# Reordering the linear attention of two images in the tail of a vision tower kernel

## The chip, the cores and the metric

The kernel runs on one core of one Trainium2 chip. The metric is the device time of one execution in microseconds, the median over runs. Engines are named PE (TensorE), DVE (VectorE), ACT (ScalarE), POOL (GpSimd) and SP (SyncE, which only issues transfers here).

## The reference

Two images of 32 channels, 128 by 128, go through a patch embedding (256 tokens of width 128), two transformer layers with linear attention, a last norm and a head of width 192. After that come one more linear attention with 12 heads of width 16, and one feed-forward block, both with residual sums. The change touches the last attention and what stands just ahead of it:

```python
h = _ln(x, lnf_g, lnf_b) @ head_w + head_b          # the head, 192 wide
# then, on the layer norm of h:
qkv = x_ @ W_qkv                                    # 192 -> 3 * 192
q, k, v = jnp.split(qkv, 3, axis=-1)
q = elu(q) + 1 ; k = elu(k) + 1                     # the features
kv = jnp.einsum('bshd,bshm->bhdm', k, v)
z = 1.0 / (jnp.einsum('blhd,bhd->blh', q, k.sum(axis=1)) + EPS)
out = jnp.einsum('blhd,bhdm,blh->blhm', q, kv, z)
h = h + (out @ W_out + b_out)
```

## The kernel before, in words

Every matmul is laid out for 128 partitions; an image is two tiles of 128 tokens. The program is written out by hand, one list of instructions per engine, with semaphores between them; no scheduler changes the order. An engine takes its list in the order written, and a wait in front of an instruction holds everything behind it on that engine.

The two images are interleaved. In the tail, image 0 is some steps ahead of image 1. For each image `i` the steps are:

- last norm: DVE adds the feed-forward result (`add_ff`), takes moments (`moments`, `mean_and_variance`), and centres (`centre`); PE transposes (`turn`, L327), a gain is multiplied on (`gain`, L1519, on ACT before), PE multiplies by the head (`head`, L440); POOL computes the inverse deviation (L1782), and DVE scales and adds the head's offset (`head_rows`, L1023), which gives `h`.
- norm of `h`: `moments3`, `mean_and_variance`, `centre` on DVE; `turn3` (L332) on PE. The transposed rows are split in a rounded high part and a low part (`high_part3`, `rest_low_part3`, `low_part3` on DVE, one copy of a rest on ACT), so that fast matmuls give full precision.
- projection: `qk3_high` and `qk3_low` give queries and keys of a tile in one bank, `v3_rows` the values.
- features: elu + 1 is computed as max(min(exp, 1), x + 1): `phi3_exp` (L1551) and `phi3_plus_one` (L1555) on ACT read the bank, `phi3_max` (L1037) on DVE joins them. The inverse deviation is applied as their scale.
- attention: `turn_heads` transposes queries, `context3` is keys times values, `context3_masked` and `context3_sums` (DVE) keep the blocks of each head, `numerators3` multiplies by the queries; `denominator3`, `inverse3`, `attention3` (DVE) divide; `turn_heads` again, a copy on ACT, and `attend3` (L489) is the output projection.

Then follow the residual sum, another norm and the feed-forward block (`fc3`, `proj3`), image 0 first.

Semaphores that matter below: `centred3`, `high3`, `low3` (norm and parts of an image are ready), `qk3_done`, `phi3_exp_ready`, `phi3_plus_one_ready`, `phi3_ready`, `context3_ready`, `attention3_ready`, `attention3_columns` (the copy in front of `attend3`).

Of the kernel before, what the change touches and what calls it, by code (L numbers as in the profile page):

```python
# [8 lines left out]
ALU = mybir.AluOpType  # L9
# [6 lines left out]
TOKENS = (SIDE // PATCH) ** 2  # L16
# [8 lines left out]
E = 192  # L25
# [32 lines left out]
def build(nc, small, convb, norm_rows0, norm_rows1, embed0, patches1, qkv_w, rest_w, rows, mix, fc_w, proj_w,  # L58
          head_w, aqkv_w, aout_w, out):
    with ExitStack() as ctx:  # L60
# [3 lines left out]
        def sem(name):  # L64
            return ctx.enter_context(nc.semaphore(name))
# [58 lines left out]
        def bias_row(name, n=0, width=D):  # L124
# [128 lines left out]
            sem(n) for n in ("y_ready", "y_turned",))  # L253
        consts_set = sem("consts_set")
# [52 lines left out]
        def _(pe):  # L307
# [518 lines left out]
            qk3_low(0, 0).then_inc(qk3_done, 1)  # L826
            pe.wait_ge(centred_last, 4)
            turn(TURNF_BANK[1], xn[1]).then_inc(last_turned, 1)
            qk3_low(0, 1).then_inc(qk3_done, 1)
            pe.wait_ge(head_in_ready, 2)  # L830
            head(1, 0).then_inc(head_done, 1)
            head(1, 1).then_inc(head_done, 1)
            v3_rows(0, 0).then_inc(v3_done, 1)
            v3_rows(0, 1).then_inc(v3_done, 1)
# [4 lines left out]
            pe.wait_ge(centred3, 4)  # L839
            pe.wait_ge(q3_columns, 1)  # L840
            turn3(TURN3_BANK[1], TURN3_REST_BANK[1], xn[1]).then_inc(turned3, 1)
            pe.wait_ge(context3_ready, 2)
            numerators3(0).then_inc(numerators3_done, 1)
            pe.wait_ge(high3, 2)
            qk3_high(1, 0)
            pe.wait_ge(low3, 2)
            qk3_low(1, 0).then_inc(qk3_done, 1)
            qk3_high(1, 1)
            pe.wait_ge(attention3_ready, 2)
            turn_heads(AT3_BANK[0], att3[0]).then_inc(attention3_turned, 1)  # L850
            qk3_low(1, 1).then_inc(qk3_done, 1)
# [75 lines left out]
        def _(dve):  # L927
# [106 lines left out]
            def rest_low_part3(i, bankof):  # L1034
                return low_part(yT3_rest[i][EB:P, :], bankof[0:EB, 0:TOKENS], yT3_rest[i][0:EB, :])

# [373 lines left out]
            centre(1, 1, x, D).then_inc(centred_last, 1)  # L1410
            dve.wait_ge(phi3_plus_one_ready, 1)
            phi3_max(0, 0).then_inc(phi3_ready, 1)
# [5 lines left out]
            dve.wait_ge(phi3_exp_ready, 2)  # L1418
            phi3_max(0, 1).then_inc(phi3_ready, 1)
            head_rows(1, 1).then_inc(h_ready, 1)  # L1420
            dve.wait_ge(moments3_done, 3)
# [8 lines left out]
            dve.wait_ge(context3_done, 1)  # L1430
            context3_masked(0).then_inc(context3_ready, 1)
            context3_sums(0).then_inc(context3_ready, 1)
            dve.wait_ge(turned3, 2)
            high_part3(1, TURN3_BANK[1]).then_inc(high3, 1)
            dve.wait_ge(rest_high3, 2)
            rest_low_part3(1, TURN3_REST_BANK[1])
            dve.wait_ge(high3, 2)
            low_part3(1, TURN3_BANK[1]).then_inc(low3, 1)
# [3 lines left out]
            inverse3(0).then_inc(inverse3_ready, 1)  # L1442
# [530 lines left out]
```

## Time and profile before

| what | value |
|---|---|
| median of 3 runs | 130.71 us (130.52 to 131.06) |
| the profiled execution | 130.16 us, its span 128.4 us |
| PE busy | 117.3 us (91%) |
| DVE busy | 75.5 us (59%) |
| ACT busy | 63.8 us (50%) |
| POOL busy | 48.7 us (38%) |
| granted clock of TensorE | 1.00 |

The span is what lies between the first and the last instruction of the trace; the rest of an execution's time, 1.76 us here, lies around it. All times of rows are counted from the span's start. Engines overlap, so the shares add up to more than 100%. A busy share is a mean over all stages; in the tail, where the change is made, each engine often waits for another.

### The profile page before, as it was taken

To read this page: it belongs to the slowest core of one execution; us is meant where nothing else is said; L and a number is where in the kernel's file an instruction comes from. 1 tells how busy PE (TensorE), PEld (TensorE's weight loads), DVE (VectorE), ACT (ScalarE), POOL (GpSimd) and SP (SyncE) were. 2 spreads that over 40 slices of the span, in tenths; PEclk is the share of its full clock that TensorE was granted. 3 is DMA by queue.
4 is the path that set the end of the run, shared out by engine and by line. 5 is a ranking of instruction groups with operands and counts; after the bars stand their busy time and mean duration, and the time that the engine had idled before them with its cause. 6 is when DMAs were issued, how large, how long until landed. Compare 5 with 4: busy or idle time off the path is not lost.

```text
span 128.4 us, 2242 instructions
## 1 busy us (share of the span) xinstructions
PE 117.3 (91%) x852; PEld 101.4 (79%) x852; DVE 75.5 (59%) x236; ACT 63.8 (50%) x151; POOL 48.7 (38%) x60
## 2 busy tenths in 40 slices
PE   6999969999999999998999798769889988999991
PEld 6999968986976798996856687757588777998990
DVE  5000384988678963779999866348588477155002
ACT  3000153745578586477774459633872835423520
POOL 0000024043896584416759546096309022032000
PEclk9999999999999999999999999999999999999999
DMA  4999899999100000000000000000000000000101
GB/s 106 373 428 416 242 434 370 406 421 398 50 0 0 0 3 5 0 0 0 0 0 5 0 0 3 0 5 3 0 0 0 0 0 5 0 0 0 61 0 61
DMA packets 3884, 12.18 MB, mean 95 GB/s; under 512 B 441, under 2 KB 1817, under 8 KB 3618
## 3 DMA queue, kind: packets, MB, share of 16 engines
q1 hardware_dynamic: 3874, 12.05, 24.8%
q8 instruction: 6, 0.10, 0.3%
q14 instruction: 4, 0.03, 0.1%
HBM read 11.65 MB, written 0.39 MB: 94 GB/s over the span
## 4 chain that ended last, share of the span: by engine, by line
PE 60%; DVE 14%; DMA 9%; ACT 7%; POOL 4%; issue 3%; SPq 3%; DVEq 0%; POOLq 0%
DMA norm_rows_sb<-in_norm_rows 9%; PE bank L505 6%; PE bank L376 4%; PE bank L419 4%; PE bank L400 4%; PE bank L320 3%; SPq L262 3%; PE bank L341 3%; PE bank L371 3%; PE bank L393 2%; PE bank L353 2%; PE bank L491 2%; PE bank L329 2%; PE bank L407 2%; POOL rstd L1782 2%
## 5 line engine op out<-in xcount | busy, mean ns | idle before, releaser
L1782 POOL TENSOR_TENSOR rstd<-mv,minus_half 128x2 f32<-128x2 f32 x14 | 10.0, 714 | 39.4 <-DVE mv L935 39.1
L1800 POOL TENSOR_TENSOR qn<-q,rqsum 128x512 f32<-128x512 f32 x8 | 8.3, 1044 | 12.3 <-DVE rqsum L995 12.3
L1566 ACT ACTIVATE patches_sb<-bank,fcb 128x256 f32<-128x256 f32 x12 | 5.1, 471 | 10.5 <-PE bank L502 10.5
L1524 ACT ACTIVATE kexp<-bank,nkmax 128x256 f32<-128x256 f32 x16 | 7.5, 472 | 5.7 <-DVE nkmax L975 5.7
L419 PE MATMUL bank<-restw,hid 128*128 128x128 f32 x64 | 8.8, 281 | 1.0 <-ACT hid L1540 1.0
L505 PE MATMUL bank<-projw,patches_sb 128*128 128x192 f32 x48 | 9.4, 331 | 0.0
L400 PEld LDWEIGHTS bank<-cw,qT 128*128 128x128 f32 x64 | 7.8, 192 | 1.6 <-issue 1.0
L419 PEld LDWEIGHTS bank<-restw,hid 128*128 128x128 f32 x64 | 7.8, 191 | 1.6 <-ACT hid L1540 1.4
L400 PE MATMUL bank<-cw,qT 128*128 128x128 f32 x64 | 8.4, 277 | 0.4 <-DVE x L1010 0.4
L320 PEld LDWEIGHTS bank<-embed_sb 128*128 128x128 f32 x64 | 8.1, 203 | 0.1
L320 PE MATMUL bank<-embed_sb 128*128 128x128 f32 x64 | 8.2, 285 | 0.0
L1540 ACT ACTIVATE hid<-bank,small_sb 128x256 f32<-128x256 f32 x16 | 6.5, 473 | 3.2 <-PE bank L414 3.2
L505 PEld LDWEIGHTS bank<-projw,patches_sb 128*128 128x128 f32 x48 | 7.6, 189 | 0.5 <-ACT patches_sb L1566 0.4
L376 PE MATMUL bank<-ktok,y 128*128 128x512 f32 x16 | 8.0, 612 | 0.0
L1514 ACT ACTIVATE x<-bank 128x128 f32<-128x128 f32 x4 | 1.1, 282 | 13.8 <-DVE stats L929 13.8
L1536 ACT ACTIVATE cw<-bank,rksum 128x128 f32<-128x128 f32 x16 | 4.8, 366 | 6.4 <-PE bank L393 5.3
L320 PE MATMUL bank<-embed_sb,patches_sb 128*128 128x128 f32 x64 | 7.9, 277 | 0.0
L929 DVE BATCH_NORM_STATS2 stats<-bank 128x6 f32<-128x128 f32 x4 | 1.1, 275 | 11.0 <-PE bank L325 11.0
L320 PEld LDWEIGHTS bank<-embed_sb,patches_sb 128*128 128x128 f32 x64 | 7.5, 192 | 0.1
L975 DVE TENSOR_REDUCE nkmax<-bank 128x2 f32<-128x512 f32 x8 | 5.4, 688 | 3.0 <-PE bank L360 2.9
L1792 POOL TENSOR_TENSOR xb<-x,rows_sb 128x256 f32<-128x256 f32 x8 | 5.9, 737 | 1.9 <-DVE y L944 1.2
L311 PE MATMUL bank<-ones 128*128 128x192 f32 x16 | 5.2, 487 | 1.1 <-DVE stats L1083 1.1
(167 smaller groups left out, 335.5 us busy)
## 6 DMA issues: line engine op xcount, KB each, us to landing
embed_sb<-in_embed SPq DMA_DIRECT2D x3, 768.0 KB, 6.9
patches_sb<-in_patches SPq DMA_DIRECT2D x2, 1024.0 KB, 11.9
restw<-in_rest_w SPq DMA_DIRECT2D x2, 768.0 KB, 16.5
qkvw<-in_qkv_w SPq DMA_DIRECT2D x3, 256.0 KB, 11.1
qkvw<-in_qkv_w SPq DMA_DIRECT2D x1, 768.0 KB, 16.6
fcw<-in_fc_w SPq DMA_DIRECT2D x1, 768.0 KB, 19.1
embed_sb<-in_embed SPq DMA_DIRECT2D x1, 576.0 KB, 4.3
aqkvw<-in_aqkv_w SPq DMA_DIRECT2D x1, 576.0 KB, 11.8
```

The costliest lines, as they stand in the source:

```text
L311: mm = nc.tensor.matmul(dst[:, 0:E], ones[:, 0:P], ones[:], start=True, stop=True)
L320: mm = nc.tensor.matmul(CONV_BANK[i][t][:, 0:D], left, embed_sb[:, c, 0:D], start=(c == 0), stop=False)
L376: return nc.tensor.matmul(YK_BANK[s][:], y[s % IMAGES][:, t, :], ktok[:, t, :], start=(t == 0), stop=(t == TILES - 1))
L400: mm = nc.tensor.matmul(ATT_BANK[s][t][:, 0:D], qT[:, t, c * P:(c + 1) * P], cw[:, c, :], start=(c == 0), stop=(c == PAIRS - 1))
L419: mm = nc.tensor.matmul(FF2_BANK[s][t][:, 0:D], hid[:, c, t * P:(t + 1) * P], ff2w(s // IMAGES, c), start=(c == 0), stop=(c == FC - 1))
L505: return nc.tensor.matmul(PROJ3_BANK[i][t][:, 0:E], hid3[i][:, c, t * P:(t + 1) * P], projw[:, c, :], start=(c == 0), stop=(c == HC - 1))
L975: return nc.vector.tensor_reduce(nkmax[i][:, 2 * b:2 * b + 2], K_BANK[s][b][:].rearrange("p (c t) -> p c t", c=2), AX_X, ALU.max, negate=True)
L1524: return nc.scalar.activation(kexp[:, c, :], K_BANK[s][c // 2][:, (c % 2) * TOKENS:(c % 2 + 1) * TOKENS], ACT.Exp, bias=nkmax[i][:, c:c + ...
L1540: return nc.scalar.activation(hid[:, c, :], FF1_BANK[s][c // 2][:, (c % 2) * TOKENS:(c % 2 + 1) * TOKENS], ACT.Gelu, bias=col("ff1_b", s / ...
L1782: return nc.gpsimd.tensor_tensor(rstd[i][:], mv[i][:, :, 1], minus_half[:], ALU.pow)
L1792: return nc.gpsimd.tensor_tensor(xb[i][:], x[i][:], row.unsqueeze(1).to_broadcast([P, TILES, D]), ALU.add)
L1800: return nc.gpsimd.tensor_tensor(qn[:, t, :].rearrange("p (h d) -> p h d", h=HEADS), q[:, t, :].rearrange("p (h d) -> p h d", h=HEADS), rq ...
```

## The change

Only the order and the engine of some steps in the tail change; what is computed stays the same.

- PE: image 0's second low projection and both groups of its value rows stand ahead of (around) image 1's transposes and head. Image 0's numerators stand ahead of image 1's `turn3`. Of image 1's projection both high halves stand first, and both low ones behind the transposes of image 0's attention.
- DVE takes two operations over from ACT: `phi3_plus_one` of image 0's first tile and `gain` of image 1. Both maxima of image 0 stand ahead of image 1's head rows. The masks of image 0's context stand ahead of the rest of image 1's moments and its centring. Image 0's denominator and inverse stand behind image 1's high part, and ahead of its rest part; image 1's low part stands behind image 0's attention.
- ACT: without the two operations; `phi3_exp` of image 0's second tile stands ahead of its `phi3_plus_one`.

```diff
@@ PE
             qk3_low(0, 0).then_inc(qk3_done, 1)
+            qk3_low(0, 1).then_inc(qk3_done, 1)
+            v3_rows(0, 0).then_inc(v3_done, 1)
             pe.wait_ge(centred_last, 4)
             turn(TURNF_BANK[1], xn[1]).then_inc(last_turned, 1)
-            qk3_low(0, 1).then_inc(qk3_done, 1)
-            pe.wait_ge(head_in_ready, 2)
+            v3_rows(0, 1).then_inc(v3_done, 1)
+            pe.wait_ge(head_in_second, 1)
             head(1, 0).then_inc(head_done, 1)
             head(1, 1).then_inc(head_done, 1)
-            v3_rows(0, 0).then_inc(v3_done, 1)
-            v3_rows(0, 1).then_inc(v3_done, 1)
...
-            pe.wait_ge(centred3, 4)
             pe.wait_ge(q3_columns, 1)
-            turn3(TURN3_BANK[1], TURN3_REST_BANK[1], xn[1]).then_inc(turned3, 1)
             pe.wait_ge(context3_ready, 2)
             numerators3(0).then_inc(numerators3_done, 1)
+            pe.wait_ge(centred3, 4)
+            turn3(TURN3_BANK[1], TURN3_REST_BANK[1], xn[1]).then_inc(turned3, 1)
             pe.wait_ge(high3, 2)
             qk3_high(1, 0)
-            pe.wait_ge(low3, 2)
-            qk3_low(1, 0).then_inc(qk3_done, 1)
             qk3_high(1, 1)
             pe.wait_ge(attention3_ready, 2)
             turn_heads(AT3_BANK[0], att3[0]).then_inc(attention3_turned, 1)
+            pe.wait_ge(low3, 2)
+            qk3_low(1, 0).then_inc(qk3_done, 1)
             qk3_low(1, 1).then_inc(qk3_done, 1)
@@ DVE, the new helpers
+            def gain(i, bankof):
+                return nc.vector.tensor_scalar(yT[i][:], bankof[:, 0:TOKENS], col("lnf_g"), None, ALU.mult)
+
+            def phi3_plus_one(i, t):
+                return nc.vector.tensor_scalar(qk3p[i][:, t, :], QK3_BANK[i][t][:, 0:2 * E], rstd[i][:, t:t + 1], 1.0,
+                                               ALU.mult, ALU.add)
@@ DVE
+            dve.wait_ge(deviation3_ready, 1)
+            dve.wait_ge(phi3_exp_ready, 1)
+            phi3_plus_one(0, 0).then_inc(phi3_plus_one_first, 1)
+            dve.wait_ge(last_turned, 2)
+            gain(1, TURNF_BANK[1]).then_inc(head_in_second, 1)
+            dve.wait_ge(phi3_plus_one_first, 1)
+            phi3_max(0, 0).then_inc(phi3_ready, 1)
             dve.wait_ge(phi3_plus_one_ready, 1)
-            phi3_max(0, 0).then_inc(phi3_ready, 1)
+            phi3_max(0, 1).then_inc(phi3_ready, 1)
...
-            dve.wait_ge(phi3_exp_ready, 2)
-            phi3_max(0, 1).then_inc(phi3_ready, 1)
             head_rows(1, 1).then_inc(h_ready, 1)
+            dve.wait_ge(context3_done, 1)
+            context3_masked(0).then_inc(context3_ready, 1)
+            context3_sums(0).then_inc(context3_ready, 1)
...
-            dve.wait_ge(rest_high3, 2)
-            rest_low_part3(1, TURN3_REST_BANK[1])
-            dve.wait_ge(high3, 2)
-            low_part3(1, TURN3_BANK[1]).then_inc(low3, 1)
             dve.wait_ge(numerators3_done, 1)
             denominator3(0).then_inc(denominator3_ready, 1)
             dve.wait_ge(denominator3_ready, 1)
             inverse3(0).then_inc(inverse3_ready, 1)
+            dve.wait_ge(rest_high3, 2)
+            rest_low_part3(1, TURN3_REST_BANK[1])
             dve.wait_ge(inverse3_ready, 1)
             attention3(0, 0).then_inc(attention3_ready, 1)
             attention3(0, 1).then_inc(attention3_ready, 1)
+            dve.wait_ge(high3, 2)
+            low_part3(1, TURN3_BANK[1]).then_inc(low3, 1)
...
-            dve.wait_ge(phi3_plus_one_ready, 4)
+            dve.wait_ge(phi3_plus_one_ready, 3)
@@ ACT
             phi3_exp(0, 0).then_inc(phi3_exp_ready, 1)
-            act.wait_ge(last_turned, 2)
-            gain(1, TURNF_BANK[1]).then_inc(head_in_ready, 1)
-            phi3_plus_one(0, 0).then_inc(phi3_plus_one_ready, 1)
             act.wait_ge(qk3_done, 2)
+            phi3_exp(0, 1).then_inc(phi3_exp_ready, 1)
             phi3_plus_one(0, 1).then_inc(phi3_plus_one_ready, 1)
-            phi3_exp(0, 1).then_inc(phi3_exp_ready, 1)
```

The line numbers of the changed kernel are shifted by 1 on PE, by up to 8 on DVE and by 13 on ACT.

VectorE, from the end of the last norm of image 1 to the masks of image 0's context (L1039 is `phi3_max`, L1024 `head_rows`, L932 and L935 moments, L952 `centre`, L1046 and L1051 the masks). Before:

```order
L1039 SCALAR_TENSOR_TENSOR embed_sb<-embed_sb 128x384 [waits phi3_plus_one_ready]
L1024 SCALAR_TENSOR_TENSOR h<-bank,rstd,head_row 128x192 [waits deviation_last_ready,head_done]
L932 BN_STATS stats<-h 128x6 [waits h_ready]
L1039 SCALAR_TENSOR_TENSOR embed_sb<-embed_sb 128x384 [waits phi3_exp_ready]
L1024 SCALAR_TENSOR_TENSOR h<-bank,rstd,head_row 128x192
L935 BN_AGGR mv<-stats 128x2 [waits moments3_done]
L932 BN_STATS stats<-h 128x6 [waits h_ready]
L935 BN_AGGR mv<-stats 128x2 [waits moments3_done]
L952 TENSOR_SCALAR xn<-h,mv 128x192
L952 TENSOR_SCALAR xn<-h,mv 128x192 [waits mean3_ready]
L1046 TENSOR_TENSOR kv<-bank,small_sb 96x2x96 [waits context3_done]
L1051 SCALAR_TENSOR_TENSOR kv<-bank,small_sb 96x2x6
```

The same place in the changed kernel, up to image 1's first aggregate (L1042 is `phi3_plus_one`, the new L1039 `gain`, L1047 `phi3_max`, L1054 and L1059 the masks):

```order
L1042 TENSOR_SCALAR embed_sb<-bank,rstd 128x384 [waits phi3_exp_ready,deviation3_ready]
L1039 TENSOR_SCALAR yT<-bank,small_sb 128x256 [waits last_turned]
L1047 SCALAR_TENSOR_TENSOR embed_sb<-embed_sb 128x384 [waits phi3_plus_one_first]
L1047 SCALAR_TENSOR_TENSOR embed_sb<-embed_sb 128x384 [waits phi3_plus_one_ready]
L1025 SCALAR_TENSOR_TENSOR h<-bank,rstd,head_row 128x192 [waits deviation_last_ready,head_done]
L933 BN_STATS stats<-h 128x6 [waits h_ready]
L1025 SCALAR_TENSOR_TENSOR h<-bank,rstd,head_row 128x192
L1054 TENSOR_TENSOR kv<-bank,small_sb 96x2x96 [waits context3_done]
L1059 SCALAR_TENSOR_TENSOR kv<-bank,small_sb 96x2x6
L936 BN_AGGR mv<-stats 128x2 [waits moments3_done]
```

Two operations came in ahead of everything, both maxima stand together ahead of the head rows, and the masks moved ahead of image 1's aggregates, second moments and centring.

VectorE, the parts of image 1's transposed rows and image 0's denominators (L1029 the high part, L962 the rest part and the low part, L1060 the denominator, L1064 the inverse, L1067 the attention). Before:

```order
L1029 CAST yT_hi<-bank 128x256 [waits turned3]
L962 TENSOR_TENSOR yT_rest<-bank,yT_rest 64x256 [waits rest_high3]
L962 TENSOR_TENSOR yT_lo<-bank,yT_hi 128x256 [waits high3]
L1060 TENSOR_SCALAR den<-bank 128x24 [waits numerators3_done]
L1064 RECIPROCAL z<-den 128x24 [waits denominator3_ready]
L1067 TENSOR_TENSOR embed_sb<-bank,z 128x192 [waits inverse3_ready]
L1067 TENSOR_TENSOR embed_sb<-bank,z 128x192
```

And in the changed kernel:

```order
L1030 CAST yT_hi<-bank 128x256 [waits turned3]
L1068 TENSOR_SCALAR den<-bank 128x24 [waits numerators3_done]
L1072 RECIPROCAL z<-den 128x24 [waits denominator3_ready]
L963 TENSOR_TENSOR yT_rest<-bank,yT_rest 64x256 [waits rest_high3]
L1075 TENSOR_TENSOR embed_sb<-bank,z 128x192 [waits inverse3_ready]
L1075 TENSOR_TENSOR embed_sb<-bank,z 128x192
L963 TENSOR_TENSOR yT_lo<-bank,yT_hi 128x256 [waits high3]
```

The low part moved from the third place to the last; the high part kept its place at the front.

TensorE, from image 0's contexts to the output projection of its attention (L469 `context3`, L334 and L335 `turn3`, L485 `numerators3`, L449 and L450 high, L452 to L454 low projection, L478 `turn_heads`, L491 `attend3`). The changed kernel, from its numerators (L486) on:

```order
L486 MATMUL bank<-kv,patches_sb 128x102 [waits context3_ready,q3_columns]
L486 MATMUL bank<-kv,patches_sb 128x102 x3
L335 MATMUL bank<-small_sb,xn 128x128 [waits centred3]
...
L450 MATMUL bank<-aqkvw_hi,yT_hi 128x384 [waits high3]
...
L479 MATMUL bank<-small_sb,embed_sb 96x128 [waits attention3_ready]
L479 MATMUL bank<-small_sb,embed_sb 96x128 x3
L453 MATMUL bank<-aqkvw_hi,yT_lo 128x384 [waits low3]
...
L492 MATMUL bank<-aoutw,qkvw 128x192 [waits loaded_aout,attention3_columns]
```

Before, the numerators stood behind image 1's transposes, and its first low projection ahead of the transposes of image 0's attention (L478); both now stand the other way round.

## Rows read from the trace of the kernel before

**Rows 1.** the page, the chain's shares of the span by engine.

```profile
PE 60%; DVE 14%; DMA 9%; ACT 7%; POOL 4%; issue 3%; SPq 3%; DVEq 0%; POOLq 0%
```

**Rows 2.** the chain of waits in order of time, tail (start us, us, what).

```profile
91.57 0.17 PE bank L453
...
95.29 0.64 PE bank L478 x4
...
99.57 0.67 ACT embed_sb L1556
...
101.24 1.58 PE bank L491 x8
```

**Rows 3.** VectorE's timeline (start us, us, what [idle before <-releaser]).

```profile
93.49 0.56 DVE L1039 SCALAR_TENSOR_TENSOR embed_sb<-embed_sb 128x384 f32<-128x384 f32 x1 [1.81 <-ACT embed_sb L1556]
93.97 0.41 DVE L1024 SCALAR_TENSOR_TENSOR h<-bank,rstd,head_row 128x192 f32<-128x192 f32 x1
...
95.48 0.18 DVE L935 BATCH_NORM_AGGREGATE mv<-stats 128x2 f32<-128x9 f32 x1
...
96.11 0.50 DVE L952 TENSOR_SCALAR xn<-h,mv 128x192 f32<-128x192 f32 x2
96.76 0.35 DVE L1046 TENSOR_TENSOR kv<-bank,small_sb 96x192 f32<-96x192 f32 x1 [0.16 <-PE bank L469]
...
97.37 0.42 DVE L1029 CAST yT_hi<-bank 128x256 fp32r<-128x256 f32 x1 [0.18 <-PE bank L335]
...
98.26 0.42 DVE L962 TENSOR_TENSOR yT_lo<-bank,yT_hi 128x256 fp32r<-128x256 f32 x1
...
99.14 0.62 DVE L1067 TENSOR_TENSOR embed_sb<-bank,z 128x192 f32<-128x192 f32 x2
```

**Rows 4.** ScalarE's timeline over the same stretch.

```profile
92.43 0.47 ACT L1520 ACTIVATE yT<-bank,small_sb 128x256 f32<-128x256 f32 x1
92.79 1.24 ACT L1556 ACTIVATE embed_sb<-bank,ones,rstd 128x384 f32<-128x384 f32 x2
93.90 0.60 ACT L1552 ACTIVATE embed_sb<-bank,rstd 128x384 f32<-128x384 f32 x1
95.00 0.73 ACT L1560 ACTIVATE v<-bank,rstd 128x192 f32<-128x192 f32 x2 [0.50 <-PE bank L454]
...
99.57 0.67 ACT L1556 ACTIVATE embed_sb<-bank,ones,rstd 128x384 f32<-128x384 f32 x1 [1.82 <-PE bank L454]
...
100.61 0.58 ACT L1514 ACTIVATE qkvw<-bank 96x512 f32<-96x512 f32 x1
```

**Rows 5.** TensorE's timeline, three parts of that stretch.

```profile
91.75 0.43 PE L329 MATMUL bank<-small_sb,xn 128*128 128x128 f32 x2
...
92.95 0.92 PE L441 MATMUL bank<-headw,yT 128*128 128x192 f32 x4 [0.24 <-ACT yT L1520]
...
94.58 0.27 PE L453 MATMUL bank<-aqkvw_hi,yT_rest 128*128 128x192 f32 x1
94.69 0.27 PE L454 MATMUL bank<-aqkvw_lo,yT_rest 128*128 128x192 f32 x1
...
97.25 1.14 PE L485 MATMUL bank<-kv,patches_sb 96*128 96x102 f32 x8
...
98.74 0.44 PE L452 MATMUL bank<-aqkvw_hi,yT_lo 128*128 128x384 f32 x1
...
99.82 0.64 PE L478 MATMUL bank<-small_sb,embed_sb 128*96 128x128 f32 x4
```

**Rows 6.** GpSimd's timeline.

```profile
98.70 1.01 POOL L1796 TENSOR_TENSOR hb<-h,rows_sb 128x384 f32<-128x384 f32 x1
```

**Rows 7.** TensorE's level: a stretch with gaps, and the first matmuls.

```profile
80.00:84.00 4.00, 2.52 (x20) 2.31 (x20) 1.85 (x7) 2.52 (x6) 0.44 (x1) 1.00 0.00 0
...
4.70 1.49 PE L311 MATMUL bank<-ones 128*128 128x192 f32 x4
...
7.38 0.82 PE L311 MATMUL bank<-ones 128*128 128x192 f32 x4
```

More of the change, by code:

```diff
@@ L253, in build @@
             sem(n) for n in ("y_ready", "y_turned",))
+        phi3_plus_one_first, head_in_second = sem("phi3_plus_one_first"), sem("head_in_second")
         consts_set = sem("consts_set")
@@ L1429, in _ @@
             centre(1, 1, h, E).then_inc(centred3, 1)
-            dve.wait_ge(context3_done, 1)
-            context3_masked(0).then_inc(context3_ready, 1)
-            context3_sums(0).then_inc(context3_ready, 1)
             dve.wait_ge(turned3, 2)
             high_part3(1, TURN3_BANK[1]).then_inc(high3, 1)
-            dve.wait_ge(rest_high3, 2)
-            rest_low_part3(1, TURN3_REST_BANK[1])
-            dve.wait_ge(high3, 2)
-            low_part3(1, TURN3_BANK[1]).then_inc(low3, 1)
             dve.wait_ge(numerators3_done, 1)
```

## The prediction

> **What bounds the kernel now.** I read the page first, then the chain of waits in order of time over the tail, then the timeline of each engine there. The page gives TensorE 60% of the chain, VectorE 14% [rows 1]. That is a mean over stages. In the stretch that the change touches, the chain hops between three engines: its pieces from 95.29 on are the transposes of image 0's queries, contexts, image 1's transposes, image 0's numerators, image 1's projection, then ScalarE's two feature passes over image 1, ScalarE's copy of image 0's transposed attention, and only then, at 101.24, the output projection of image 0's attention [rows 2]. From there nothing that ends the kernel starts before that projection: image 0's sum, norm and feed-forward stage hang on it, and image 1's features were ready earlier than they are used. So the question is one number: how does the change move 101.24?
>
> Who sets 101.24: ScalarE's copy of the attention at 100.61 stands behind image 1's plus-one (99.57) and exp in ScalarE's order, and plus-one waited 1.82 us for TensorE [rows 4], which had waited for VectorE's low part of image 1, at 98.26 for 0.42 [rows 3]. The reader is to see that the time is set by **image 1's** low part, not by image 0's attention: that was ready earlier (99.14 + 0.62 = 99.76, its transposes at 99.82 for 0.64, rows 5) and then waited in front of ScalarE.
>
> The arithmetic below follows engine order: an instruction starts when its engine has come to it and its semaphore is there, some 0.03 to 0.05 us after the releaser's end; neighbours on one engine overlap by about 0.08 (the first maximum ends at 93.49 + 0.56 = 94.05, the head rows start at 93.97, rows 3).
>
> **Step 1, image 0's features (gain).** ScalarE loses gain(1) (0.47) and one plus-one (two took 1.24 together) [rows 4]. Both projections of image 0 now run without image 1's transposes between them, so the second exp follows the first at once: 92.43 instead of 93.90. Its plus-one then ends at 93.6. VectorE does the other plus-one from 92.57. Its cost (128x384 out of PSUM) has no row. Bounds: 0.42, the cast of 256 columns, and 0.67, ScalarE's own [rows 3, 4]; I take 0.55, the two-input pass over the same 384 columns in SBUF (0.56), which is the nearest. It is hidden at either end: VectorE must wait after it until image 1's transposes end. These now stand behind three projection steps of 0.17 [rows 2] and a v group of five at 0.11 (94.58 to 94.69) [rows 5], so they end not at 92.18 (91.75 + 0.43) but at 93.2. Then gain on VectorE: 0.42 by the cast of the same shape, at worst ScalarE's 0.47, at best 0.3 (a centring pass, half of 0.50 plus overlap) [rows 3, 4]. It ends at 93.68. The two maxima follow, to 94.08 and 94.63 (0.56 each, 0.48 apart). The v copies on ScalarE end at 94.6 (0.73 for both, rows 4), since the v rows end at 93.8 instead of 94.96. TensorE's transposes of the queries start at 94.68, not 95.29: **0.6 us gained** for image 0. The contexts, the masks (96.76 becomes 96.15) and the numerators (97.25 becomes 96.63, ending at 97.77) keep it [rows 3, 5].
>
> **Step 2, image 1's head and moments (loss).** The head matmuls wait for gain: 93.73 instead of 92.95, done at 94.65 [rows 5]. The first head rows on VectorE start at 94.70 instead of 93.97 (+0.73); moments and second head rows end at 95.8. Now the two mask operations stand in front of the rest. VectorE waits for them until 96.15, idle 0.35, and is past them at 96.5. From the first aggregate to the last centring it was 95.48 to 96.61 (96.11 + 0.50), 1.13 [rows 3]; now 96.51 to 97.64. That is **+1.03**. Image 1's transposes follow on TensorE at once, as before, and the cast of their high part starts at 98.40 instead of 97.37.
>
> **Step 3, the denominators (the gain of step 1 is lost).** Their code stands behind that cast on VectorE. The numerators are done at 97.8, but the cast waits for image 1's transposes and ends only at 98.82. Denominator and inverse filled the 0.46 from the low part's end (98.26 + 0.42 = 98.68) to 99.14 [rows 3]; now they run from 98.82 to 99.28. The rest part stands between them and the attention now, a pass like the low part (0.42), to 99.67; the attention then runs 99.62 to 100.25, against 99.14 to 99.76: **+0.5** for image 0, not -0.6.
>
> **Step 4, the low part of image 1 (loss).** It is moved behind the attention. Cast start to low part's end was 97.37 to 98.68, 1.31; now it has denominator, inverse and two attention products (0.62) inside, 98.40 to 100.60, 2.2: **+0.9** more. On TensorE the order fits this: transposes of the attention at 100.30, then the low projection at 100.70 against 98.74 [rows 5], where the transposes' own 0.4 makes a last 0.05 to 0.1. The sum is 1.03 + 0.89 + 0.04 = 1.96 us. ScalarE's order is unchanged there: plus-one 101.53 instead of 99.57, exp, then the attention copy, and the output projection at 103.20 instead of 101.24. The second projection's high half is now done early (0.35 of TensorE's time off the path), which saves nothing, because ScalarE is busy with the first tile's passes until the attention copy anyway.
>
> **Step 5, the rest.** After 101.24 the orders are the same row for row, and each wait there has its root in the output projection: image 0's sum, ScalarE's v copies behind the v rows, the norm's GpSimd step, the masks. GpSimd's chain behind image 1's moments (its deviation, a weight part, a row sum) moves 1 us with them and ends at 100.7 instead of 99.7 [rows 6]; its results are read after the output projection. So +1.96 goes to the end whole. The profiled execution took 130.16 us (span 128.4), which gives 132.1; the median of the runs is 130.71, 0.55 above the profiled one, and it is the median that is compared, so I forecast 130.71 + 1.96 = **132.7**. Bounds of the unpriced operations: gain at 0.30 or 0.47 moves -0.12 or +0.05; hand-overs, twelve on the path at 0.02 of error each, 0.25 either way; the plus-one nothing. The forecast's own range is 132.2 to 133.2.
>
> **The rivals.**
> A: image 1 has slack, only image 0's attention counts. Then the attention's transposes at +0.5 set the output projection: 131.2. For it: in the rows the attention was turned at 100.46, and ScalarE's copy of it started at 100.61, only 0.15 later, so the two chains are close before the change. Against it: ScalarE's order is written out, and its exp of image 1 stands in front. 6%.
> B, faster: the numerators' 0.6 us comes through to VectorE. It decides at one point, VectorE's cast at 97.37: if image 1's transposes ended by 97.8, the denominators would run at 97.85 and the attention would end 0.9 to 1.0 us earlier than 99.76, and if also ScalarE then took it before image 1's passes, the projection would start up to 1.0 us earlier: 129.7. Against it: the head's chain is later by 0.73 before any mask wait. 3%.
> C: the clock. TensorE gets new gaps: about 0.65 before the numerators, 0.75 before image 1's projection, 0.6 before the attention's transposes, 1.3 before the output projection. In this trace the granted clock stayed 1.00 after gaps of 1.0 and 0.9 within 80 to 84, with TensorE busy 2.52 of 4 us [rows 7]; that is about the density I expect between 96.6 and 103.2. At the start the same matmul with `ones` came every 0.32 us (4.70 to 5.98 for four), later every 0.163 (7.38 for 0.82) [rows 7]: the 1.2 and the 2.4 GHz level. If the clock fell in the new gaps, the eight output projection matmuls at 0.32 instead of 0.163 and the ten v rows at twice their 0.11 would add 1.3 and 1.1 at least: 135.1. 6%.
> The Trainium skill, "TensorE: Matmul & The Clock Gate", section "Part 1: The HAM clock gate (the "warmup" mystery)", says that "the default state is throttled, and activity releases the throttle", which speaks against a change that thins out TensorE's work. This case's rows show the release (0.32 to 0.163) but no fall after gaps as long.
> D: the loss is partly hidden, for example because the two VectorE operations overlap more than I take: half of step 4, 131.8 to 132.2. 8%.
>
> **How the numbers follow.** My forecast has 77%, A 6, B 3, C 6, D 8. 0.5% of 130.71 is 0.65 us, about what a measurement of this kernel can tell from no change: same is 130.06 to 131.36. Slower is the forecast, C and D (0.91), same is A (0.06), faster B (0.03). The range 131.3 to 133.8 leaves out B, most of A and C, and a little at the edges.
>
> **What would show it.** In the trace after: ScalarE's exp passes over image 0 back to back near 92.4; the query transposes near 94.7; a VectorE gap before the masks of about 0.35 and one before image 1's cast of about 0.8, ending near 98.4; the denominators directly behind that cast, not at 97.85; image 1's low part near 100.2; ScalarE idle nearly 3 us before image 1's plus-one; TensorE idle about 1.3 before the output projection, which starts near 103.2. Wrong would be a cast of image 1 before 98, or ScalarE's attention copy before 102. If all these starts are right and the end is not 1.9 to 2.1 later, step 5 is what failed.

## The result and the profile after

| | before | after |
|---|---|---|
| median | 130.81 us (130.52 to 131.06) | 132.81 us (132.57 to 133.51) |
| runs | 4 | 4 |
| after over before, 95% | | 1.0161 [1.0131, 1.0190] |
| profiled execution, its span | 130.16, 128.4 us | 133.51, 131.7 us |
| granted clock of TensorE | 1.00 | 1.00 |

The change costs 2.00 us by the medians, against 1.96 predicted; 132.81 lies in the range. The interval of the ratio allows 1.7 to 2.5 us, so the times alone can't tell 1.90 from 1.96; where tenths matter below, they are read from rows. One of the ten executions of copy_first below (134.43 us) was in a slower state of the chip: its ratio leaves that one out, and without it the median is 132.10 us, not 132.19.

The profiled execution of after is the longest of its four, and 3.35 us longer than that of before. So the first thing to settle is how much of this lies ahead of the tail. These lines are from VectorE's timeline of before and of after (start us, us, what): the cast of image 0's high part, which stands ahead of everything that the change moves, and VectorE's last pass.

```profile
89.76 0.42 DVE L1029 CAST yT_hi<-bank 128x256 fp32r<-128x256 f32 x1
...
125.49 0.68 DVE L1078 TENSOR_TENSOR embed_sb<-bank,hb 128x192 f32<-128x192 f32 x2 [7.04 <-PE bank L505]
```

```profile
91.21 0.42 DVE L1030 CAST yT_hi<-bank 128x256 fp32r<-128x256 f32 x1
...
128.84 0.68 DVE L1086 TENSOR_TENSOR embed_sb<-bank,hb 128x192 f32<-128x192 f32 x2 [7.05 <-PE bank L506]
```

Before the cast, after is 1.45 us late already; from cast to last pass it takes 37.63 us against 35.73, that is 1.90 more. The 1.45 belongs to this execution and not to the change: copy_first, below, has the same program up to that cast and reaches it at 89.66. In the execution of after TensorE waited 1.0 us for the input patches, a wait that the execution of before hasn't, which is the larger part of the 1.45. The waits of TensorE up to 45 us (what waited <- for what: us, times, longest), and the page's rows on that transfer, of after and of before (KB each, median us from issue to landing):

```profile
PE bank L321 <- DMA patches_sb<-in_patches: 1.0, 1, 1.0
```

```profile
patches_sb<-in_patches SPq DMA_DIRECT2D x2, 1024.0 KB, 13.1
```

```profile
patches_sb<-in_patches SPq DMA_DIRECT2D x2, 1024.0 KB, 11.9
```

Therefore every tail below is counted from the start of image 0's cast, in that execution itself (its anchor). VectorE in the tail of after ([rows 3] is the same of before; a bracket is idle time before the row, and its releaser):

```profile
94.09 0.62 DVE L1042 TENSOR_SCALAR embed_sb<-bank,rstd 128x384 f32<-128x384 f32 x1 [0.95 <-ACT embed_sb L1565]
94.68 0.48 DVE L1039 TENSOR_SCALAR yT<-bank,small_sb 128x256 f32<-128x256 f32 x1
95.08 1.02 DVE L1047 SCALAR_TENSOR_TENSOR embed_sb<-embed_sb 128x384 f32<-128x384 f32 x2
96.18 0.42 DVE L1025 SCALAR_TENSOR_TENSOR h<-bank,rstd,head_row 128x192 f32<-128x192 f32 x1
...
97.53 0.35 DVE L1054 TENSOR_TENSOR kv<-bank,small_sb 96x192 f32<-96x192 f32 x1 [0.23 <-PE bank L470]
...
99.71 0.42 DVE L1030 CAST yT_hi<-bank 128x256 fp32r<-128x256 f32 x1 [0.75 <-PE bank L336]
100.05 0.17 DVE L1068 TENSOR_SCALAR den<-bank 128x24 f32<-128x24 f32 x1
100.26 0.30 DVE L1072 RECIPROCAL z<-den 128x24 f32<-128x24 f32 x1
100.59 0.42 DVE L963 TENSOR_TENSOR yT_rest<-bank,yT_rest 64x256 fp32r<-64x256 f32 x1
101.02 0.62 DVE L1075 TENSOR_TENSOR embed_sb<-bank,z 128x192 f32<-128x192 f32 x2
101.56 0.41 DVE L963 TENSOR_TENSOR yT_lo<-bank,yT_hi 128x256 fp32r<-128x256 f32 x1
```

ScalarE ([rows 4]) and TensorE ([rows 5]) there, and two windows of the engines (window, length, PE busy and its instructions, PEld, DVE, ACT, POOL, granted clock, DMA share, GB/s):

```profile
94.40 0.67 ACT L1569 ACTIVATE embed_sb<-bank,ones,rstd 128x384 f32<-128x384 f32 x1
95.22 0.73 ACT L1573 ACTIVATE v<-bank,rstd 128x192 f32<-128x192 f32 x2
...
102.91 0.67 ACT L1569 ACTIVATE embed_sb<-bank,ones,rstd 128x384 f32<-128x384 f32 x1 [2.82 <-PE bank L455]
103.48 0.57 ACT L1565 ACTIVATE embed_sb<-bank,rstd 128x384 f32<-128x384 f32 x1
103.94 0.58 ACT L1527 ACTIVATE qkvw<-bank 96x512 f32<-96x512 f32 x1
```

```profile
94.26 0.38 PE L330 MATMUL bank<-small_sb,xn 128*128 128x128 f32 x2
...
96.16 0.64 PE L479 MATMUL bank<-small_sb,embed_sb 128*96 128x128 f32 x4
...
98.11 1.11 PE L486 MATMUL bank<-kv,patches_sb 96*128 96x102 f32 x8 [0.61 <-DVE kv L1059]
...
100.19 0.44 PE L450 MATMUL bank<-aqkvw_hi,yT_hi 128*128 128x384 f32 x1 [0.52 <-DVE yT_hi L1030]
...
101.70 0.64 PE L479 MATMUL bank<-small_sb,embed_sb 128*96 128x128 f32 x4 [0.55 <-DVE embed_sb L1075]
102.10 0.42 PE L453 MATMUL bank<-aqkvw_hi,yT_lo 128*128 128x384 f32 x1
...
104.58 1.57 PE L492 MATMUL bank<-aoutw,qkvw 96*128 96x192 f32 x8 [1.19 <-ACT qkvw L1527]
```

```profile
96.00:100.00 4.00, 3.04 (x25) 2.49 (x24) 2.87 (x12) 0.88 (x2) 1.39 (x2) 1.00 0.00 0
100.00:104.00 4.00, 2.65 (x14) 2.02 (x14) 1.90 (x7) 1.18 (x4) 2.03 (x2) 1.00 0.00 0
```

GpSimd's row that answers to [rows 6] starts at 9.83 from the cast, against 8.94; its result `hb` of image 1 is there at 102.03, and image 1's residual sum comes only after image 0's at 106.18:

```profile
101.04 0.99 POOL L1806 TENSOR_TENSOR hb<-h,rows_sb 128x384 f32<-128x384 f32 x1
```

The reader is to see two things. Image 0's steps come earlier (contexts and masks), then its attention does not, because denominators (L1068, L1072) wait behind the cast of image 1. And ScalarE is idle 2.82 us before image 1's plus-one, against 1.82 in [rows 4]: that is where the added time shows.

The starts, counted from image 0's cast, in us; the last two columns are the difference and what the prediction had for it:

| start of | before | after | measured | predicted |
|---|---|---|---|---|
| image 0's query transposes | 5.53 | 4.95 | -0.58 | -0.61 |
| image 1's first head rows | 4.21 | 4.97 | +0.76 | +0.73 |
| masks of image 0 | 7.00 | 6.32 | -0.68 | -0.61 |
| numerators of image 0 | 7.49 | 6.90 | -0.59 | -0.62 |
| cast of image 1's high part | 7.61 | 8.50 | +0.89 | +1.03 |
| attention of image 0 (VectorE) | 9.38 | 9.81 | +0.43 | +0.5 |
| low part of image 1 | 8.50 | 10.35 | +1.85 | +1.92 |
| image 1's plus-one (ScalarE) | 9.81 | 11.70 | +1.89 | +1.96 |
| output projection (TensorE) | 11.48 | 13.37 | +1.89 | +1.96 |
| VectorE's last pass | 35.73 | 37.63 | +1.90 | +1.96 |

### The profile page after: what moved, and what is told of

It reads as the page before. It is cut to its first block, busy times and chain, and to the rows that moved or that the text cites. A ratio compares the mean times of both kernels' runs of the same rounds, so it can differ in the third digit from the quotient of the medians.

```text
span 131.7 us, 2243 instructions
## 1 busy us (share of the span) xinstructions
PE 117.6 (89%) x852; PEld 102.0 (77%) x852; DVE 76.5 (58%) x238; ACT 62.9 (48%) x149; POOL 48.6 (37%) x60
## 4 chain that ended last, share of the span: by engine, by line
PE 57%; DVE 13%; DMA 12%; ACT 5%; SPq 5%; POOL 3%; issue 2%
DMA patches_sb<-in_patches 12%; PE bank L506 6%; SPq L263 5%; PE bank L377 4%; PE bank L420 4%; PE bank L401 3%; PE bank L321 3%; PE bank L372 2%; PE bank L394 2%; PE bank L492 2%; PE bank L330 2%; PE bank L408 2%; PE bank L342 2%; PE bank L386 2%; POOL qn L1810 2%
```

## The experiments

Two groups of four (low_part_back, low_part_alone, masks_back and copy_first; then the rest), each with the kernel before beside it (median 130.88 us over 19 runs in the first, 130.89 over 28 in the second). Those marked * start from the kernel before, the others from the changed one. The ratio is to before; it is not the quotient of the two medians, and can differ from that by 0.001. "Low part" and "projection" are starts counted from image 0's cast, in the profiled execution (before: 8.50 and 11.48; after: 10.35 and 13.37).

| kernel | median us | ratio, 95% | low part | projection |
|---|---|---|---|---|
| low_part_back | 131.77 | 1.0075 [1.0044, 1.0105] | 9.38 | 12.36 |
| low_part_alone * | 132.52 | 1.0123 [1.0082, 1.0164] | 10.19 | 13.20 |
| masks_back | 132.55 | 1.0124 [1.0089, 1.0160] | 10.28 | 13.29 |
| copy_first | 132.19 | 1.0088 [1.0057, 1.0119] | 10.35 | 12.01 |
| denominators_first | 132.49 | 1.0130 [1.0084, 1.0176] | 10.02 | 13.24 |
| features_only | 131.05 | 1.0013 [0.9989, 1.0038] | 8.78 | 11.76 |
| gain_alone * | 130.59 | 0.9968 [0.9946, 0.9991] | 8.24 | 11.22 |
| gain_and_plus_one * | 130.40 | 0.9962 [0.9939, 0.9985] | 8.25 | 11.14 |

**low_part_back.** Image 1's rest and low part stand ahead of image 0's denominators again, and its first low projection ahead of the second high one.

```diff
@@ PE
             qk3_high(1, 0)
+            pe.wait_ge(low3, 2)
+            qk3_low(1, 0).then_inc(qk3_done, 1)
             qk3_high(1, 1)
...
-            pe.wait_ge(low3, 2)
-            qk3_low(1, 0).then_inc(qk3_done, 1)
@@ DVE
             high_part3(1, TURN3_BANK[1]).then_inc(high3, 1)
+            dve.wait_ge(rest_high3, 2)
+            rest_low_part3(1, TURN3_REST_BANK[1])
+            dve.wait_ge(high3, 2)
+            low_part3(1, TURN3_BANK[1]).then_inc(low3, 1)
             dve.wait_ge(numerators3_done, 1)
             denominator3(0).then_inc(denominator3_ready, 1)
...
-            dve.wait_ge(rest_high3, 2)
-            rest_low_part3(1, TURN3_REST_BANK[1])
...
-            dve.wait_ge(high3, 2)
-            low_part3(1, TURN3_BANK[1]).then_inc(low3, 1)
```

> The changed kernel with step 4 undone: image 1's rest and low parts stand directly behind its high part again, ahead of image 0's denominator, and its first low projection ahead of the transposes of image 0's attention. My theory (image 1's low part sets the output projection, through ScalarE's order): the low part ends 0.9 to 1.0 us earlier although image 0's attention ends 0.45 later; 1.0 faster than the changed kernel, 1.1 slower than before, about 131.8. Rival A (only image 0's attention counts): 0.45 slower than the changed kernel, about 133.2.

131.77 us: of the 2.0 us lost, 1.0 came back, as the forecast's split says (the intervals of the two ratios don't touch). In its trace image 0's attention is late by more than in after, and yet the projection is earlier. VectorE of this run:

```profile
98.73 0.42 DVE L1030 CAST yT_hi<-bank 128x256 fp32r<-128x256 f32 x1 [0.75 <-PE bank L336]
...
99.61 0.42 DVE L963 TENSOR_TENSOR yT_lo<-bank,yT_hi 128x256 fp32r<-128x256 f32 x1
...
100.50 0.62 DVE L1075 TENSOR_TENSOR embed_sb<-bank,z 128x192 f32<-128x192 f32 x2
```

From its anchor (90.23) the attention starts at 10.27 (after 9.81, before 9.38), and the projection at 12.36, against 13.37. The kernel with the later attention ends sooner; so it is image 1's low part that sets the projection, and rival A, by which only image 0's attention counts, is out.

**low_part_alone.** The same edit the other way round, made alone on the kernel before.

> The kernel before with step 4 alone: image 0's denominator, inverse and attention between image 1's high part and its low part, the low projection of image 1 behind the transposes of the attention. Numerators end at 98.4 here, 1.0 after the cast's start, so VectorE also waits for them: the low part ends 1.6 us later than before, 1.6 slower, 132.4. Rival A (only image 0's attention counts, which is at most 0.2 later): same as before within 0.2.

132.52 us. It fits the first theory and not rival A. But with low_part_back it shows something neither had said: put in alone, the edit costs 1.7 us (projection 13.20 against 11.48); taken out of the full change it gives back 1.0 (12.36 against 13.37), and the rest of the change costs 0.9 (12.36 against 11.48). The row that explains it, VectorE of this run (anchor 90.17):

```profile
97.79 0.42 DVE L1029 CAST yT_hi<-bank 128x256 fp32r<-128x256 f32 x1 [0.18 <-PE bank L335]
98.84 0.18 DVE L1060 TENSOR_SCALAR den<-bank 128x24 f32<-128x24 f32 x1 [0.63 <-PE bank L485]
...
100.36 0.41 DVE L962 TENSOR_TENSOR yT_lo<-bank,yT_hi 128x256 fp32r<-128x256 f32 x1
```

The denominators wait 0.63 us for the numerators here, and the low part, now behind them, waits too. In after the numerators are earlier, the cast is later, and that wait is gone. Alone the two losses are 1.7 and 0.9, together 1.9: they share 0.7 us.

**masks_back.** The masks stand behind image 1's centring again, and its transposes ahead of the numerators on TensorE (the diff shows VectorE's part).

```diff
             head_rows(1, 1).then_inc(h_ready, 1)
-            dve.wait_ge(context3_done, 1)
-            context3_masked(0).then_inc(context3_ready, 1)
-            context3_sums(0).then_inc(context3_ready, 1)
...
             centre(1, 1, h, E).then_inc(centred3, 1)
+            dve.wait_ge(context3_done, 1)
+            context3_masked(0).then_inc(context3_ready, 1)
+            context3_sums(0).then_inc(context3_ready, 1)
```

> The changed kernel with the mask move of step 2 undone on VectorE and TensorE: masks of image 0's context behind image 1's centring, image 1's transposes ahead of image 0's numerators. My theory: image 1's cast starts 0.75 earlier, the masks 0.65 later, but numerators now also end later (98.6), so the denominators wait for them; the low part ends 0.3 earlier: 0.3 faster, 132.5. Rival (the mask move costs all of the 1.03 of step 2): 1.0 faster, 131.8.

132.55 us, the number that was expected, but not by the gain that was expected: the low part was to come 0.3 us earlier and comes 0.07 earlier (10.28 against 10.35), and the last pass 0.06. The 0.26 us between the medians are not told apart from nothing (the intervals overlap). Image 1's cast is 0.61 us earlier than in after (7.89 against 8.50; 0.75 was expected), and next to nothing of it arrives. VectorE again waits for the numerators, which stand behind image 1's transposes:

```profile
98.14 0.42 DVE L1030 CAST yT_hi<-bank 128x256 fp32r<-128x256 f32 x1 [0.41 <-PE bank L336]
99.01 0.18 DVE L1068 TENSOR_SCALAR den<-bank 128x24 f32<-128x24 f32 x1 [0.45 <-PE bank L486]
```

Once the low part stands behind the attention, the later of the two images' chains sets it.

**features_only.** Both edits back: what is left is the early features and the two operations on VectorE.

> The changed kernel with steps 2 to 4 undone: only the first part of the change is left (image 0's projections and values ahead of image 1's transposes and head, two operations on VectorE, both maxima ahead of the head rows). My theory: image 0's query transposes 0.6 earlier, image 1's first head rows 0.7 later; the masks 0.1 later than before and image 1's low part 0.3 later, so 0.3 slower than before, 131.2; 1.7 faster than the changed kernel. Rival (the early features are worth their 0.6): 0.5 faster than before, 130.4.

The code is that of after with the diffs of low_part_back and masks_back in it. 131.05 us, not told apart from before (its interval holds 1). In the trace the cast and the projection are 0.28 us later than before (7.89 against 7.61; 11.76 against 11.48). So the cast's +0.89 is 0.28 from the first part of the change and 0.61 from the masks and numerators in front. The 0.28 is a difference of two: the first head rows start 0.76 later (at 94.84, anchor 89.87), and the second maximum, which now stands ahead of them, no longer lies between them and the first aggregate (1.04 us later, where it was 1.51 before). The 0.6 us by which image 0's queries are earlier (4.94 against 5.53) give nothing to the end: they are gone at the masks, which stand behind image 1's centring here (7.06 against 7.00).

**denominators_first.** In the order of after, denominators and attention of image 0 stand ahead of the cast of image 1's high part, so that nothing of image 1 holds them.

```diff
-            dve.wait_ge(turned3, 2)
-            high_part3(1, TURN3_BANK[1]).then_inc(high3, 1)
             dve.wait_ge(numerators3_done, 1)
             denominator3(0).then_inc(denominator3_ready, 1)
...
             inverse3(0).then_inc(inverse3_ready, 1)
-            dve.wait_ge(rest_high3, 2)
-            rest_low_part3(1, TURN3_REST_BANK[1])
             dve.wait_ge(inverse3_ready, 1)
             attention3(0, 0).then_inc(attention3_ready, 1)
             attention3(0, 1).then_inc(attention3_ready, 1)
+            dve.wait_ge(turned3, 2)
+            high_part3(1, TURN3_BANK[1]).then_inc(high3, 1)
+            dve.wait_ge(rest_high3, 2)
+            rest_low_part3(1, TURN3_REST_BANK[1])
             dve.wait_ge(high3, 2)
             low_part3(1, TURN3_BANK[1]).then_inc(low3, 1)
```

> The changed kernel with image 0's denominator, inverse and attention ahead of image 1's high part on VectorE, so that they run as soon as the numerators are there (97.8). If step 3 (the denominators stuck behind the cast) is what costs, the attention ends 1.2 earlier and the time falls by 0.5 or more, to 132.3 or less. My theory: image 1's cast now starts 0.5 later, TensorE's transposes of the attention still stand behind image 1's high projection and ScalarE's copy behind its passes over image 1; the low part ends 0.2 earlier (it loses the rest of what stood between), 0.2 faster, 132.6.

132.49 us. VectorE and ScalarE of this run (anchor 90.37):

```profile
98.97 0.62 DVE L1075 TENSOR_TENSOR embed_sb<-bank,z 128x192 f32<-128x192 f32 x2
99.51 0.41 DVE L1030 CAST yT_hi<-bank 128x256 fp32r<-128x256 f32 x1
...
100.39 0.42 DVE L963 TENSOR_TENSOR yT_lo<-bank,yT_hi 128x256 fp32r<-128x256 f32 x1
```

```profile
101.94 0.67 ACT L1569 ACTIVATE embed_sb<-bank,ones,rstd 128x384 f32<-128x384 f32 x1 [2.71 <-PE bank L455]
```

The attention starts at 8.60, 1.21 us ahead of after and 0.78 ahead of before: here the gain of step 1 is real. The low part comes 0.33 us sooner than in after, but the end moves by only 0.13 at the projection and 0.18 at the last pass: the cast is 0.64 us later now (9.14 against 8.50), and TensorE's high projections wait for it (idle 1.16), so that the transposes and the low projection come behind them. The interval of this ratio and that of after overlap, so by the times alone nothing is told apart; the rows show that at most 0.2 us hung on step 3. TensorE's wait in this run:

```profile
99.98 0.44 PE L450 MATMUL bank<-aqkvw_hi,yT_hi 128*128 128x384 f32 x1 [1.16 <-DVE yT_hi L1030]
```

**copy_first.** In ScalarE's order of after, the copy of image 0's attention stands ahead of image 1's two feature passes.

```diff
+            act.wait_ge(attention3_turned, 1)
+            evict(attT3[0].rearrange("p c t -> p (c t)"), AT3_BANK[0][0:EC, 0:ECH * TOKENS]).then_inc(attention3_columns, 1)
             act.wait_ge(qk3_done, 3)
             phi3_plus_one(1, 0).then_inc(phi3_plus_one_ready, 1)
             phi3_exp(1, 0).then_inc(phi3_exp_ready, 1)
-            act.wait_ge(attention3_turned, 1)
-            evict(attT3[0].rearrange("p c t -> p (c t)"), AT3_BANK[0][0:EC, 0:ECH * TOKENS]).then_inc(attention3_columns, 1)
```

> The changed kernel with ScalarE's copy of image 0's transposed attention ahead of its plus-one and exp of image 1. The copy then starts at once behind the transposes, and the output projection 1.3 us earlier than in the changed kernel. Step 5 as I wrote it (only the output projection's start counts): 1.3 faster, 131.4. Rival: image 1's features now come up to 1.9 us after the projection's start instead of along with it, its value copies and contexts wait, and image 1 gives back half: 0.6 faster than the changed kernel, 132.2.

132.19 us, and step 5 as it was written (131.4) is refuted. The projection starts 1.36 us sooner than in after (12.01 against 13.37), at +0.53 to before, which is what rival A had for it (+0.5), and yet the last pass is at +1.27 to before. The chain of waits of copy_first, in order of time (start us, us, what), shows who took it, and the same stretch of after and before the old order:

```profile
102.02 0.94 ACT embed_sb L1565 x2
102.96 0.57 ACT embed_sb L1569
...
103.56 0.56 DVE embed_sb L1047
104.12 0.53 DVE h L1082 x2
```

```profile
104.58 1.58 PE bank L492 x8
...
106.18 0.62 DVE h L1082 x2
```

```profile
102.25 0.56 DVE L1039 SCALAR_TENSOR_TENSOR embed_sb<-embed_sb 128x384 f32<-128x384 f32 x1 [0.94 <-ACT embed_sb L1556]
102.84 0.62 DVE L1074 TENSOR_TENSOR h<-bank,hb 128x192 f32<-128x192 f32 x2
```

The first is copy_first, the second after, the third VectorE's timeline of before. Image 0's residual sum (L1082, before L1074) stands on VectorE behind image 1's second maximum (L1047, before L1039). In before the maximum ends at 102.81 and the projection at 101.24 + 1.58 = 102.82 [rows 2]: a tie within 0.01 us. In after the order of ScalarE is unchanged and the tie moves as one. In copy_first the projection starts at 89.66 + 12.01 = 101.67, takes 1.47 us and is done at 103.14, while the maximum ends at 104.12: the sum waits 0.98 us for an operation of image 1 that it needs nothing from. The rival's number (132.2) came out, its place did not: it had image 1's value copies and contexts waiting, and it is image 0's residual sum that waits.

**gain_alone.** On the kernel before, only the gain of image 1 goes to VectorE.

```diff
@@ PE
             qk3_low(0, 1).then_inc(qk3_done, 1)
-            pe.wait_ge(head_in_ready, 2)
+            pe.wait_ge(head_in_second, 1)
@@ DVE, behind the centring of the last norm of image 1
+            dve.wait_ge(last_turned, 2)
+            gain(1, TURNF_BANK[1]).then_inc(head_in_second, 1)
@@ ACT
-            act.wait_ge(last_turned, 2)
-            gain(1, TURNF_BANK[1]).then_inc(head_in_ready, 1)
```

> The kernel before with gain of image 1 on VectorE and nothing else. VectorE is idle for 1.8 us there; gain starts at 92.2 instead of 92.43, and ScalarE's plus-one and exp of image 0 come 0.47 earlier less the second tile's wait. Both images move forward by 0.25: 0.25 faster than before, 130.6. Rival (ScalarE's copies were hidden anyway): no difference.

130.59 us, 0.32% [0.09, 0.54] faster. VectorE was idle there and takes the gain as soon as image 1's transposes are done, where on ScalarE it stood behind image 0's first exp [rows 4]. The head rows start 0.26 us earlier (3.95 against 4.21), and 0.26 arrives at the projection. VectorE of this run:

```profile
93.58 0.48 DVE L1039 TENSOR_SCALAR yT<-bank,small_sb 128x256 f32<-128x256 f32 x1 [0.53 <-PE bank L330]
```

**gain_and_plus_one.** Beside it, image 1's first plus-one (not image 0's) goes to VectorE, the pass of ScalarE ahead of the attention copy at 99.57 in [rows 4].

```diff
@@ DVE
+            dve.wait_ge(deviation3_ready, 2)
+            phi3_plus_one(1, 0).then_inc(plus_one_dve, 1)
+            dve.wait_ge(plus_one_dve, 1)
             phi3_max(1, 0).then_inc(phi3_ready, 1)
-            dve.wait_ge(phi3_plus_one_ready, 4)
+            dve.wait_ge(phi3_plus_one_ready, 3)
@@ ACT
-            phi3_plus_one(1, 0).then_inc(phi3_plus_one_ready, 1)
```

> The kernel before with gain of image 1 on VectorE, and image 1's first plus-one (not image 0's) on VectorE too, where VectorE is idle for 1.0 us. ScalarE then reaches the copy of image 0's attention behind one pass over image 1 instead of two, so the copy starts with the transposes' end: another 0.1 over gain alone, 0.35 faster than before, 130.5. Rival (order changes of a tenth of a microsecond do not reach the end): as gain alone.

130.40 us, 0.38% [0.15, 0.61] faster than before: the lowest median of all, below both kernels, but not told apart from gain_alone. ScalarE and VectorE of this run:

```profile
99.61 0.58 ACT L1565 ACTIVATE embed_sb<-bank,rstd 128x384 f32<-128x384 f32 x1 [1.81 <-PE bank L455]
100.55 0.59 ACT L1527 ACTIVATE qkvw<-bank 96x512 f32<-96x512 f32 x1 [0.36 <-PE bank L479]
```

```profile
100.22 0.62 DVE L1042 TENSOR_SCALAR embed_sb<-bank,rstd 128x384 f32<-128x384 f32 x1 [0.41 <-ACT embed_sb L1565]
```

The copy no longer waits for ScalarE but for TensorE's transposes (idle 0.36), so of the 0.57 us that the plus-one takes in ScalarE's order (start to start, 102.91 to 103.48 in after) 0.08 reach the projection. The next wait sets the rest.

## Why the prediction was right, step by step

**Step 1** held: image 0's queries are 0.58 us earlier, its numerators 0.59 (0.61 and 0.62 predicted). Two of its terms were too small. Plus-one took 0.62, not 0.55, and gain 0.48, not 0.42. The first was said to be hidden at either end. It was, with next to nothing to spare: it ended at 94.09 + 0.62 = 94.71, which with the 0.08 us by which neighbours overlap lets the next one start at 94.63, and image 1's transposes ended at 94.26 + 0.38 = 94.64; gain started at 94.68. The second stood on image 1's path and was paid for: 0.06 more than taken, of which 0.03 are left in the head rows (+0.76 for +0.73), because gain itself started 0.03 sooner than worked out (3.47 from the anchor against 3.50).

**Step 2** is the term that was too large: +1.03 for the cast, measured +0.89. The masks came 0.07 us sooner than worked out (VectorE idle 0.23, not 0.35), and from the first aggregate to the end of the centring it took 97.89 to 98.96, 1.07, not 1.13. features_only and masks_back split it into 0.28 and 0.61. This, less what step 4 gives back, is the 0.07 at the projection: -0.14 here, +0.06 in step 4 (cast start to low part's end 2.26, 99.71 to 101.97, not 2.2), the rest rounding.

**Step 3** was right as a row (attention +0.43 for +0.5) and nearly without weight for the end: denominators_first takes 1.21 us off the attention and 0.2 off the end. The prediction did not charge it to the sum, and that was right.

**Step 4** held: low_part_back puts it at 1.01 us (12.36 against 13.37) for 0.89 + 0.04. The last link also came as written there, with the transposes' own time at the end: TensorE starts the four transposes at 101.70 and the low projection at 102.10, the same 0.40 apart as 99.82 and 100.22 in before, where nothing is waited for, while the low part had ended at 101.97. So in after it is, by less than 0.1 us, the transposes of image 0's attention and not the low part that come last, and both stand behind that attention. "Image 1's low part sets the time" is true of before and of low_part_back; in after, image 0's attention lies on image 1's path, because the order puts it there. But the working reads as if step 2 and step 4 were two prices that add up whatever else is done. They are a sum in this kernel only. Alone the low part costs 1.7; the masks, taken back, give 0.06 at the last pass. Standing behind the attention, the low part waits for the later of the two images' chains, and the later one differs between these kernels.

**Step 5** gave the right number by a reason that is wrong in part. That +1.96 goes whole to the end is confirmed (1.89 at the projection, 1.90 at the end). That image 1's features were ready earlier than used, and only the projection's start counts, is refuted by copy_first. In before both ended within 0.01 us of each other; the chain of waits shows one of them only [rows 2]. Here the forecast was lucky: it had not looked at the second maximum. The number survived because the order of ScalarE from plus-one to the last maximum is the same before and after, and all of it hangs on image 1's low projection.

**The rivals.** A is out by low_part_back and low_part_alone. B is out by the cast at 8.50. denominators_first even gives image 0 what B asked for on VectorE, and at most 0.2 us come of it; the attention is then 0.78 us ahead of before, not 0.9 to 1.0, since denominator, inverse and attention from 97.85 end at 98.93 by B's own rows. B's second condition, the copy ahead of ScalarE's passes, was run only by itself (copy_first); the two together were not run. C, the clock: the gaps came (0.61, 0.52, 0.55 and 1.19 us), TensorE was busy 2.65 of 4 us in 100 to 104, about as in [rows 7], and the granted clock of the profiled executions stayed 1.00. That column alone would prove little: it reads 1.00 from 4.00 to 6.00 as well, where the matmuls with `ones` still come every 0.32 us [rows 7]. The matmuls themselves settle it: the eight of the output projection take 1.57 us in after as in before, and the value rows behind it come every 0.11 us in both. The Trainium skill, "TensorE: Matmul & The Clock Gate", section "Part 1: The HAM clock gate (the "warmup" mystery)", has activity release the throttle; the release was kept here at this density, and no run here shows how thin the work must be to lose it. C is out for the medians and not for every execution: three executions had a mean granted clock of 0.986 or 0.987 and were 1.1 to 2.2 us above the median of their kernel (one each of low_part_back, denominators_first and copy_first), among 46 of the changed kernel and those that start from it; none of the 47 of before beside them, nor of the 28 of the kernels marked *, was below 0.998. None of the three is a profiled execution, so whether the new gaps bring this about is not shown. D, a part of step 4 hidden, would have been 131.8 to 132.2; the median is above, and low_part_back shows the whole of step 4 paid.

What stays open: why the input patches are waited for in some executions and not in others (below), whether the lower clock of three executions comes from the change, and whether denominators_first is better than after by its 0.2 us.

## What to carry to other kernels

When two interleaved chains share an engine whose order is written out, ask of each moved instruction which chain is the later one at that place: time given to the earlier chain (0.6 us to image 0 here) was worth nothing, and a step of the later one put behind it cost in full (1.0 us). Prices of such moves do not add up over edits, so measure a move within the order in which it will stand. And before naming the one instruction that sets the rest, look for a second that ends at nearly the same time (0.01 us apart here): the chain of waits shows only one of a tie.

## What the runs showed of the hardware

- VectorE from PSUM, one tensor and a value for each partition: 0.62 us for 128x384 (L1042), 0.48 for 128x256 (L1039), where the plain cast of 128x256 took 0.42 [rows 3]. ScalarE took 0.67 for the 384 columns and 0.47 for the 256 [rows 4], so moving them from one engine to the other changed the place, and the length by 0.05 us at most. The Trainium skill, "VectorE: DVE Perf Modes", section "The TRN2 errata — SBUF-src ops pay a fixed extra latency per instruction", prices a PSUM source at 120 cycles and one for each element at 0.96 GHz: by estimate 0.39 us for 256 columns and 0.53 for 384. The cast is near that, the two operations with a value for each partition are 0.09 above.
- The time up to image 0's cast varies by more than most of the edits here are worth: 91.21 us in after, 91.12 in gain_alone and 89.66 in copy_first, whose programs are the same up to there. Much of it goes with TensorE's wait for the input patches: 1.0 us in after, 1.1 in gain_alone, 0.5 in denominators_first (cast at 90.37) and 0.3 in low_part_back (90.23), and none in copy_first and before (89.76); but masks_back has none either and its cast is at 90.25, so it is not all. Without counting from an anchor, gain_alone's profiled span (129.5 us) would have read as slower than before (128.4), where 0.3 us faster is measured.
